# Moving the addition of a rotary embedding from GpSimd to VectorE

## The chip, the cores and the metric

The kernel runs on one core of a Trainium2 chip. The metric is the device time of one execution in microseconds (us). Before the change it was 1877.25 us, the median of three runs (1873.11 to 1878.32).

The engines of the core are called by their names here and by short names in the rows: TensorE (PE, its weight loads PEld), VectorE (DVE), ScalarE (ACT), GpSimd (POOL) and SyncE (SP, which only issues transfers; its queue is SPq).

## The reference, cut to what matters

The model is a "macaron": a feed-forward block, an attention block and the same feed-forward block again, on 2048 tokens of 128 features.

```python
x = x + 0.5 * ffn(layernorm(x), ...)    # ffn = attention with rope, then a mixture of 8 experts (top 2)
x = x + attn(layernorm(x), ...)         # attention with rope
x = x + 0.5 * ffn(layernorm(x), ...)

# in each of the three, with 16 heads of 8 features:
q, k, v = h @ wq, h @ wk, h @ wv
q = q * cos + rotated(q) * sin          # the rotation: two products and their sum; k likewise
scores = q @ k.T / sqrt(8)              # causal
out = softmax(scores) @ v
```

So all three layers contain the same attention, and the rotation (two products, one sum) stands in each.

## The kernel before, in words

The kernel loops three times over one body (layer 0, 1, 2). One pass has a head, the attention itself and, in layers 0 and 2, the experts.

**The head** works on four chunks c of 512 tokens. TensorE turns the normalised tokens (line 776) and multiplies them by four weight matrices, for q, q with its halves exchanged, k and k exchanged (line 785), and by the matrix for v (line 793). There are 8 items i = 2c + which, where which is 0 for q and 1 for k. Each item is a tile of 128 rows (head and feature) by 512 tokens. It is rotated, and then split into three bf16 parts, whose sum carries nearly the precision of f32, so that TensorE can form the scores in bf16. For item i the steps are:

1. two multiplies by VectorE (line 581): out of PSUM, plus a bias, times the table of cosines or sines, into two f32 tiles `terms(i)`, of which there are four pairs in turn;
2. the addition of the two by GpSimd (line 684), which signals `rotated`;
3. rounding the sum to bf16 by ScalarE (line 742), part 0;
4. the remainder, sum minus part 0, by VectorE (line 571, function `remainder`);
5. rounding the remainder by ScalarE (line 725, `second`), part 1;
6. remainder minus part 1 by GpSimd (line 678, `third`), part 2, which signals `part2_ready`.

Each engine executes its instructions in the order written. VectorE does the multiplies of item i and then remainder i - 2. GpSimd does addition i and then third part i - 2. ScalarE does second i - 2 and then part 0 of item i; between them it copies the turned tokens (line 729) and v (line 744) out of PSUM. From item 4 on VectorE waits for third part i - 4 before it writes `terms(i)`, as these tiles are used again.

SyncE stores the parts of chunk c to HBM, q (line 500) after third part 2c and k (lines 502 and 504) after third part 2c + 1. From the second chunk on it then loads chunk c - 1 back in the layout of the attention, with six transfers (line 385). So the load of chunk 0 stands behind the stores of chunk 1. The load of chunk 3 stands behind the first maxout (below).

**The attention** follows a list of events that a planner writes out before, from assumed costs; all engines walk the same list, and the change touches neither its costs nor its order. Its first events are row maxima: scores by TensorE (lines 821 and 824, which wait for the load of chunk 0 and for the v copy) and a maximum by VectorE (line 609). After all of a chunk's maxima comes "maxout": TensorE transposes them (line 830), VectorE splits them into three bf16 parts (lines 624 to 628), and they go through HBM into three rows of the operand qa. Then come the scores (line 867), the exponentials (ScalarE, line 759) and the products with v (line 880). The tiles `m3` and `mr` that the maxout writes lie in the same memory as `terms`. GpSimd, when its third parts are done, clears the guard rows of the second operand buffer (line 691).

Of the kernel before, what the change touches and what calls it, by code (L numbers as in the profile page):

```python
# [8 lines left out]
ALU = mybir.AluOpType  # L9
# [9 lines left out]
NC = T // CH  # L19
# [147 lines left out]
def macaron_kernel(nc, x_in, w5, b4, vecs, wo_w, rope, router, w_gate, w_up, w_down, out):  # L167
# [16 lines left out]
    def tmp(n):  # L184
        return arena[:, n * CH:(n + 1) * CH]
# [77 lines left out]
    def sem(name):  # L263
        s = nc.alloc_semaphore(name)
        sems.append(s)
        return s
# [14 lines left out]
    terms_ready = sem("terms_ready")  # L281
    rotated = sem("rotated")
# [3 lines left out]
    part2_ready = sem("part2_ready")  # L286
# [78 lines left out]
    def terms(i):  # L365
        return tmp(2 * (i % 4)), tmp(2 * (i % 4) + 1)

    def parts(i):
        return pbuf[i % PB].bitcast(BF16).rearrange("p (l t) -> p l t", l=3)
# [100 lines left out]
    with nc.Fori(0, NLAYER) as layer:  # L470

        with nc.Block() as block:
# [73 lines left out]
            def _(dve):  # L546
# [21 lines left out]
                def remainder(i):  # L568
                    rotation, rest = terms(i)
                    dve.wait_ge(part0_ready, i + 1)  # L570
                    dve.tensor_tensor(rest, rotation, parts(i)[:, 0, :], ALU.subtract).then_inc(remainder_ready, 1)

                for i in range(2 * NC):
                    c, which = i // 2, i % 2
                    if which == 0:
                        dve.wait_ge(table_loaded[c], 16)
                    if i >= 4:
                        dve.wait_ge(part2_ready, i - 3)
                    for k in (0, 1):
                        dve.wait_ge(projected, 2 * i + k + 1)  # L580
                        dve.scalar_tensor_tensor(terms(i)[k], ps[:, 2 + 2 * which + k, :],
                                                 b4s[:, 2 * which + k:2 * which + k + 1], rtab[:, k, c * CH:(c + 1) * CH],
                                                 ALU.add, ALU.mult).then_inc(terms_ready, 1)
                    if i >= 2:
                        remainder(i - 2)
                remainder(2 * NC - 2)
# [12 lines left out]
                for ev in events:  # L599
                    kind = ev[0]  # L600
                    if kind in ("rowmax", "maxout", "normalise", "turn", "project"):
                        bank = SB + mi % MB
                        mi += 1
                        dve.wait_ge(filler_ready, mi)
                    if kind == "rowmax":
                        _, j, qt, h0, some, kc, final = ev
                        g, c = chunks[j]
                        w = min(CH, (TPC * c + qt + 1) * 128 - kc * CH)
                        dve.tensor_reduce(mpart[:, j % MD, h0:h0 + some, qt, kc],  # L609
                                          ps[:, bank, 0:some * w].rearrange("p (h w) -> p h w", h=some),  # L610
                                          axis=AX.X, op=ALU.max).then_inc(filler_used, 1)
                        if final:
                            dve.wait_ge(filler_used, mi)
                            if j >= MD:
                                dve.wait_ge(guard_split, j - MD + 1)
                            dve.tensor_reduce(mx[:, j % MD, :], mpart[:, j % MD, :, :, 0:c + 1].rearrange("p h q c -> p (h q) c"), axis=AX.X,
                                              op=ALU.max, negate=True).then_inc(maxima_ready, 1)
                    elif kind == "maxout":

                        j = ev[1]  # L620
                        if j >= MD:
                            dve.wait_ge(guard_ready[j % MD], 16 * (j // MD))
                        src = ps[0:16, bank, 0:128]
                        link(dve.tensor_copy(m3[:, j % MD, 0, :], src))
                        dve.tensor_tensor(mr, src, m3[:, j % MD, 0, :], ALU.subtract).then_inc(filler_used, 1)
                        dve.wait_ge(filler_used, mi)
                        link(dve.tensor_copy(m3[:, j % MD, 1, :], mr))
                        dve.tensor_tensor(m3[:, j % MD, 2, :], mr, m3[:, j % MD, 1, :],
                                          ALU.subtract).then_inc(guard_split, 1)
                    elif kind == "normalise":  # L630
                        j = ev[1]
                        g, c = chunks[j]
                        turned = ps[:, bank, :].rearrange("p (q h r) -> p q h r", q=TPC, r=32)
                        link(dve.reciprocal(rden[:, :, :, :], turned[:, :, :, HD:HD + 1]))  # L634
                        dve.tensor_tensor(
                            onat[:, TPC * c:TPC * (c + 1), 32 * g:32 * g + 32].rearrange("p q (h i) -> p q h i", i=HD),
                            turned[:, :, :, 0:HD], rden[:, :, :, :].broadcast_to([128, TPC, HPG, HD]),
                            ALU.mult).then_inc(filler_used, 1)
                        dve.wait_ge(filler_used, mi)
                        dve.engine_nop().then_inc(output_normalised, 1)  # L640
                    elif kind == "turn":
                        c = ev[1]
                        dve.tensor_scalar(hT[:, c * CH:(c + 1) * CH], ps[:, bank, :], wos[:, D:D + 1], None,
                                          ALU.add).then_inc(filler_used, 1)
                    elif kind == "project":
                        c = ev[1]
                        rows = slice(TPC * c, TPC * (c + 1))
                        y = rec[:, 0, :].rearrange("p (t d) -> p t d", d=D)
                        dve.tensor_tensor(y, ps[:, bank, :].rearrange("p (t d) -> p t d", d=D),
                                          vbc[:, V_BO:V_BO + 1, :].broadcast_to([128, TPC, D]),  # L650
                                          ALU.add).then_inc(filler_used, 1)
                        dve.wait_ge(filler_used, mi)

                        if c == 0:
                            dve.wait_ge(x1_ready, TT)
                        with dve.If(layer == 1):
                            dve.tensor_tensor(xs[:, rows, :], xs[:, rows, :], y, ALU.add).then_inc(residual_added, 1)
                            dve.wait_ge(residual_added, c + 1)
                            for t in range(TPC * c, TPC * (c + 1)):
                                dve.bn_stats(stats[:, t, :], xs[:, t, :]).then_inc(stats_ready, 1)  # L660
                            dve.wait_ge(stats_ready, TPC * (c + 1))
                            for t in range(TPC * c, TPC * (c + 1)):
                                dve.bn_aggr(mv[:, t, :], stats[:, t, :]).then_inc(squares_done, 1)
                        with dve.If(layer != 1):
                            dve.tensor_tensor(x1[:, rows, :], x1[:, rows, :], y, ALU.add).then_inc(residual_added, 1)
                            dve.wait_ge(residual_added, c + 1)
                            for k in range(TPC):
                                t = TPC * c + k
                                dve.tensor_tensor_reduce(rec[:, 1, k * D:(k + 1) * D], x1[:, t, :], x1[:, t, :],
                                                         1.0, 0.0, ALU.mult, ALU.add, rst[:, 2, t:t + 1]  # L670
                                                         ).then_inc(squares_done, 1)
                        dve.wait_ge(squares_done, TPC * (c + 1))

            @block.gpsimd
            def _(pool):
                def third(i):
                    pool.wait_ge(part1_ready, i + 1)
                    pool.tensor_tensor(parts(i)[:, 2, :], terms(i)[1], parts(i)[:, 1, :],
                                       ALU.subtract).then_inc(part2_ready, 1)

                for i in range(2 * NC):
                    rotation, other = terms(i)
                    pool.wait_ge(terms_ready, 2 * i + 2)
                    pool.tensor_tensor(rotation, rotation, other, ALU.add).then_inc(rotated, 1)
                    if i >= 2:
                        third(i - 2)
                third(2 * NC - 2)
                third(2 * NC - 1)

# [7 lines left out]
                for ev in events:  # L697
                    if ev[0] == "scores":
                        _, s, j, kt, h = ev
# [614 lines left out]
```

## Time and profile before

| | |
|---|---|
| profiled execution | 1875.36 us |
| its span (first to last instruction) | 1873.8 us |
| TensorE busy | 1660.0 us, 89% |
| VectorE busy | 1364.7 us, 73% |
| ScalarE busy | 1104.4 us, 59% |
| GpSimd busy | 441.7 us, 24% |
| mean granted TensorE clock | 0.914 of full |

How to read it: the shares are means over the whole span, and the head of a layer is a short stretch of it (the first is at 12 to 44 us), so the rows below look at that stretch alone. The busy time of an instruction includes what it waits for inside the engine, such as memory that another engine holds. "Idle before" in brackets is how long the engine had nothing to do and what ended it. The granted clock is the share of TensorE's full speed that the chip allowed.

### The profile page before, as it was taken

The page shows a single profiled execution, that of the slowest core. Times are in us where ns is not written, and L with a number is a line of the kernel's source. Part 1 is how long each engine was busy: PE and PEld are TensorE (multiplying, and loading weights), DVE is VectorE, ACT ScalarE, POOL GpSimd, SP SyncE. Part 2 cuts the span into 40 slices and gives each one's busy share as a digit, 9 for nine tenths or more (in the row PEclk, how much of TensorE's full clock was granted, in tenths as well). Part 3 has the DMA queues.
Part 4 walks back from the last instruction along what each step waited for, and adds up shares of the span by engine and source line. Part 5 has one row for each costly group of instructions (what it writes and reads, how often), then busy time and mean ns, then how long its engine had stood idle before and what let it go on. Part 6 is the DMA issues. An engine that isn't in the chain of part 4 may idle for free. (4 is left out here: it accounts for less than half of the span.)

```text
span 1873.8 us, 31585 instructions
## 1 busy us (share of the span) xinstructions
PE 1660.0 (89%) x11190; PEld 769.0 (41%) x11190; DVE 1364.7 (73%) x2862; ACT 1104.4 (59%) x2304; POOL 441.7 (24%) x491
## 2 busy tenths in 40 slices
PE   5899999999849947899999999579999999994795
PEld 3333333333239933333333332233333333423795
DVE  7888998987153348889999983388899999825333
ACT  5355777767716624457777778234576777782463
POOL 6003201111016735031101020150311010200574
PEclk9788999999959977889999999778899999995898
DMA  5400203300011134200202000142002020001113
GB/s 163 108 1 3 52 3 105 68 2 2 8 33 44 47 100 141 52 2 2 53 2 52 2 2 2 61 141 52 2 7 47 2 53 2 1 2 30 35 47 89
DMA packets 63581, 75.92 MB, mean 41 GB/s; under 512 B 13656, under 2 KB 56221, under 8 KB 62105
## 3 DMA queue, kind: packets, MB, share of 16 engines
q1 hardware_dynamic: 54184, 62.13, 13.1%
q0 software_dynamic: 4992, 9.40, 2.1%
q10 hardware_dynamic: 4224, 2.10, 0.4%
q8 instruction: 99, 1.62, 0.4%
q14 instruction: 82, 0.66, 0.1%
HBM read 53.05 MB, written 21.46 MB: 40 GB/s over the span
## 5 line engine op out<-in xcount | busy, mean ns | idle before, releaser
L759 ACT ACTIVATE probs<-ps 128x512 f32<-128x512 f32 (+3 forms) x1920 | 879.0, 543 | 471.3 <-PE ps L867 469.8
L609 DVE TENSOR_REDUCE mpart<-ps 128x1 f32<-128x512 f32 (+3 forms) x1680 | 1014.4, 665 | 115.6 <-PE ps L821 65.3
L821 PE MATMUL ps<-ka,qa 96*128 96x512 bf16 (+3 forms) x1920 | 669.6, 371 | 36.5 <-DMA ka<-ksplit 23.1
L867 PE MATMUL ps<-qa,ka 96*128 96x512 bf16 (+3 forms) x1920 | 616.2, 357 | 1.5 <-DMA qa<-guard 0.9
L880 PE MATMUL ps<-probs,vv 128*9 128x512 f32 (+3 forms) x3840 | 442.5, 533 | 8.8 <-ACT probs L759 8.1
L708 POOL TENSOR_SCALAR_AFFINE_SELECT probs<-probs 128x512 f32<-128x512 f32 x192 | 122.0, 635 | 1168.7 <-ACT probs L759 1168.7
L821 PEld LDWEIGHTS ps<-ka,qa 96*128 96x128 bf16 x1920 | 191.8, 100 | 480.3 <-DVE mpart L609 335.6
L867 PEld LDWEIGHTS ps<-qa,ka 96*128 96x128 bf16 x1920 | 183.4, 99 | 187.7 <-ACT probs L759 69.2
L824 PE MATMUL ps<-mask_rows,identb 128*128 128x128 bf16 x768 | 161.6, 235 | 0.0
L1215 DVE TENSOR_TENSOR probs<-probs,ps 112x512 f32<-112x512 f32 x78 | 53.6, 687 | 144.5 <-ACT probs L1183 144.5
L1140 PE MATMUL ps<-hT,probs 128*112 128x128 f32 x1248 | 152.7, 277 | 2.9 <-ACT probs L1170 1.9
L1140 PEld LDWEIGHTS ps<-hT,probs 128*112 128x112 f32 x1248 | 144.9, 180 | 4.2 <-ACT probs L1170 2.2
L880 PEld LDWEIGHTS ps<-probs,vv 128*9 128x9 f32 x3840 | 57.7, 88 | 158.4 <-ACT probs L759 118.3
L1170 ACT ACTIVATE probs<-wgu 128x896 f32 x78 | 74.1, 950 | 66.4 <-PEq L886 38.5
L1074 POOL DMA_INDIRECT arena<-tokens,from_row x78 | 76.9, 986 | 115.7 <-issue 69.5
L634 DVE RECIPROCAL rden<-ps 128x16 f32<-128x16 f32 x48 | 11.9, 249 | 113.2 <-PE ps L835 113.0
L1084 POOL DMA_INDIRECT results<-hT,to_row x78 | 78.5, 1007 | 59.3 <-issue 30.7
L824 PEld LDWEIGHTS ps<-mask_rows,identb 128*128 128x128 bf16 x768 | 80.3, 105 | 28.9 <-issue 2.0
L1152 PE MATMUL ps<-wds,probs 112*128 x624 | 82.8, 275 | 1.5 <-DVE probs L1215 1.4
L1152 PEld LDWEIGHTS ps<-wds,probs 112*128 112x128 f32 x624 | 75.8, 192 | 2.3 <-issue 2.3
L1163 ACT ACTIVATE hT<-ps 128x128 f32<-128x128 f32 x78 | 21.6, 277 | 61.6 <-PE ps L1124 61.6
L776 PE MATMUL ps<-identf,onat 128*128 128x128 f32 x48 | 9.1, 321 | 54.2 <-DVE onat L562 54.2
(166 smaller groups left out, 943.6 us busy)
## 6 DMA issues: line engine op xcount, KB each, us to landing
qa<-qsplit SPq DMA_DIRECT2D x27, 384.0 KB
ka<-ksplit SPq DMA_DIRECT2D x27, 384.0 KB
probs<-rope SPq DMA_DIRECT2D x12, 512.0 KB, 6.3
qa<-qsplit SPq DMA_DIRECT2D x36, 96.0 KB
ka<-ksplit SPq DMA_DIRECT2D x36, 96.0 KB
qsplit<-arena SPq DMA_DIRECT2D x6, 384.0 KB, 3.0
ksplit<-arena SPq DMA_DIRECT2D x6, 384.0 KB, 2.8
tokens<-arena SPq DMA_DIRECT2D x2, 1024.0 KB, 8.0
```

Source lines behind the costliest of these rows:

```text
L609: dve.tensor_reduce(mpart[:, j % MD, h0:h0 + some, qt, kc], ps[:, bank, 0:some * w].rearrange("p (h w) -> p h w", h=some), axis=AX.X, op=A ...
L708: pool.affine_select(out=own, in_=own, compare_op=ALU.is_ge, fill=0.0, base=0, pattern=[[0, HPG], [1, 128]], channel_multiplier=-1).then_i ...
L759: act.activation(probs[:, s % 2, h, 0:n], ps[:, u % SB, 0:n], ACT.Exp, scale=SCALE).then_inc(probs_ready, 1)
L821: ins = pe.matmul(dst, qa[0:KROWS, b, h0 + k, tile * 128:(tile + 1) * 128], ka[0:KROWS, b, h0 + k, kc * CH:kc * CH + n], start=True, stop= ...
L824: ins = pe.matmul(dst[:, n - 128:n], identb[:, :], mask_rows[:, :], start=False, stop=True)
L867: pe.matmul(dst, ka[0:KROWS, b, h, kt * 128:(kt + 1) * 128], qa[0:KROWS, b, h, c * CH + q0:(c + 1) * CH], start=True, stop=True).then_inc( ...
L880: ins = pe.matmul(ps[32 * h:32 * h + HD + 1, SB + MB, q0:CH], vv[:, kt, g * HPG + h, :], probs[:, s % 2, h, 0:CH - q0], start=kt == 0, sto ...
L1074: pool.indirect_dma_start(xring[:, u % XR, :], None, tokens, bass.IndirectOffsetOnAxis(ap=from_row[:, u:u + 1], axis=0)).then_inc(tile_loa ...
L1084: pool.indirect_dma_start(results, bass.IndirectOffsetOnAxis(ap=to_row[:, u:u + 1], axis=0), obuf[:, u % OR, :], None, bounds_check=TOPK * ...
L1140: ins = pe.matmul(ps[0:MR, 2 * (i % 2) + b, k * 128:(k + 1) * 128], wcur[:, i % 2, b * M + k * MR:b * M + (k + 1) * MR], xt[:, i % 2, :], ...
L1152: ins = pe.matmul(ps[:, 4 + u % 2, 0:D], atb[u % 2][:, k * 128:(k + 1) * 128], wds[0:MR, bass.ds(experts[u], 1), k, :].rearrange("p o d -> ...
L1170: act.activation(wcur[:, u % 2, :], wgu[:, bass.ds(expert, 1), :].rearrange("p o m -> p (o m)"), ACT.Copy).then_inc(expert_copied, 1)
```

## The change: what it does

VectorE executes the addition itself, right behind the two multiplies of the same item, after a wait for its own second multiply. GpSimd loses the addition and executes only the eight third parts. Since the order of GpSimd no longer guarantees that third parts are done before the maxout overwrites the memory of `terms`, VectorE waits for all eight before the first maxout. ScalarE, TensorE and SyncE have the same instructions and waits as before.

```diff
--- before.py
+++ after.py
@@ -581,6 +581,9 @@
                         dve.scalar_tensor_tensor(terms(i)[k], ps[:, 2 + 2 * which + k, :],
                                                  b4s[:, 2 * which + k:2 * which + k + 1], rtab[:, k, c * CH:(c + 1) * CH],
                                                  ALU.add, ALU.mult).then_inc(terms_ready, 1)
+                    rotation, other = terms(i)
+                    dve.wait_ge(terms_ready, 2 * i + 2)
+                    dve.tensor_tensor(rotation, rotation, other, ALU.add).then_inc(rotated, 1)
                     if i >= 2:
                         remainder(i - 2)
                 remainder(2 * NC - 2)
@@ -618,6 +621,8 @@
                     elif kind == "maxout":
 
                         j = ev[1]
+                        if j == 0:
+                            dve.wait_ge(part2_ready, 2 * NC)
                         if j >= MD:
                             dve.wait_ge(guard_ready[j % MD], 16 * (j // MD))
                         src = ps[0:16, bank, 0:128]
@@ -678,12 +683,8 @@
                     pool.tensor_tensor(parts(i)[:, 2, :], terms(i)[1], parts(i)[:, 1, :],
                                        ALU.subtract).then_inc(part2_ready, 1)
 
-                for i in range(2 * NC):
-                    rotation, other = terms(i)
-                    pool.wait_ge(terms_ready, 2 * i + 2)
-                    pool.tensor_tensor(rotation, rotation, other, ALU.add).then_inc(rotated, 1)
-                    if i >= 2:
-                        third(i - 2)
+                for i in range(2 * NC - 2):
+                    third(i)
                 third(2 * NC - 2)
                 third(2 * NC - 1)
```

## Rows read from the trace of the kernel before

**Rows 1.** the page, part 1: busy us (share of span), instructions.

```profile
PE 1660.0 (89%) x11190; PEld 769.0 (41%) x11190; DVE 1364.7 (73%) x2862; ACT 1104.4 (59%) x2304; POOL 441.7 (24%) x491
```

**Rows 2.** windows: length; busy of PE, PEld, DVE, ACT, POOL; granted clock; DMA.

```profile
27.30:45.20 17.90, 9.94 (x45) 6.04 (x44) 14.28 (x14) 11.12 (x18) 17.63 (x14) 0.84 0.64 195
...
44.00:60.00 16.00, 12.91 (x59) 5.84 (x60) 13.97 (x27) 0.96 (x1) 4.63 (x3) 0.61 0.74 198
60.00:600.00 540.00, 493.66 (x3340) 211.90 (x3338) 404.17 (x831) 333.11 (x712) 95.76 (x116) 0.92 0.14 32
```

**Rows 3.** timeline: start, duration, engine, line, operation [idle before]; heads of layers 0, 1.

```profile
17.36 0.75 DVE L581 SCALAR_TENSOR_TENSOR arena<-ps,b4s,probs 128x512 f32<-128x512 f32 x1 [0.45 <-PE ps L785]
...
44.26 0.26 PE L821 MATMUL ps<-ka,qa 96*128 96x128 bf16 x1 [7.96 <-DMA ka<-ksplit]
...
695.78 0.75 DVE L581 SCALAR_TENSOR_TENSOR arena<-ps,b4s,probs 128x512 f32<-128x512 f32 x1 [0.44 <-PE ps L785]
...
722.69 0.26 PE L821 MATMUL ps<-ka,qa 96*128 96x128 bf16 x1 [7.56 <-DMA ka<-ksplit]
```

**Rows 4.** timeline of SyncE's queue in the head of layer 0.

```profile
36.45 0.36 SPq L502 DMA_DIRECT2D ksplit<-x  x1
...
40.06 0.38 SPq L385 DMA_DIRECT2D ka<-ksplit  x1
...
46.30 0.38 SPq L385 DMA_DIRECT2D ka<-ksplit  x1
```

**Rows 5.** timeline of GpSimd in the head of layer 0.

```profile
27.33 1.16 POOL L678 TENSOR_TENSOR arena<-arena 128x512 bf16<-128x512 f32 x1 [0.95 <-ACT arena L725]
28.45 1.27 POOL L684 TENSOR_TENSOR arena<-arena 128x512 f32<-128x512 f32 x1
...
32.48 1.15 POOL L678 TENSOR_TENSOR rec<-arena,rec 128x512 bf16<-128x512 f32 x1
...
35.27 1.16 POOL L678 TENSOR_TENSOR x<-arena,x 128x512 bf16<-128x512 f32 x1
...
43.97 1.15 POOL L678 TENSOR_TENSOR rec<-arena,rec 128x512 bf16<-128x512 f32 x1
```

**Rows 6.** timeline of ScalarE in the head of layer 0.

```profile
26.63 0.62 ACT L725 ACTIVATE arena<-arena 128x512 bf16<-128x512 f32 x1
...
34.22 0.63 ACT L725 ACTIVATE x<-arena 128x512 bf16<-128x512 f32 x1 [1.03 <-DVE arena L571]
...
41.45 0.58 ACT L744 ACTIVATE vv<-ps 128x512 f32<-128x512 f32 x1
```

**Rows 7.** by line, whole span: count, duration ns min/median/max, first and last start.

```profile
L684 POOL TENSOR_TENSOR arena<-arena x24: 1264/1680/1727, 19.8 to 1230.1; 128x512 f32<-128x512 f32 x24
...
L678 POOL TENSOR_TENSOR x<-arena,x x6: 1144/1150/1167, 35.3 to 1229.0; 128x512 bf16<-128x512 f32 x6
...
L571 DVE TENSOR_TENSOR arena<-arena x12: 678/1114/1748, 24.6 to 1230.6; 128x512 f32<-128x512 f32 x12
...
L581 DVE SCALAR_TENSOR_TENSOR arena<-ps,b4s,probs x48: 732/743/752, 17.4 to 1228.5; 128x512 f32<-128x512 f32 x48
```

**Rows 8.** timeline of VectorE in the head of layer 0.

```profile
25.16 1.40 DVE L581 SCALAR_TENSOR_TENSOR arena<-ps,b4s,probs 128x512 f32<-128x512 f32 x2
26.48 0.68 DVE L571 TENSOR_TENSOR arena<-arena 128x512 f32<-128x512 f32 x1
28.58 1.41 DVE L581 SCALAR_TENSOR_TENSOR arena<-ps,b4s,probs 128x512 f32<-128x512 f32 x2 [1.42 <-POOL arena L678]
...
32.62 1.55 DVE L571 TENSOR_TENSOR arena<-arena,x 128x512 f32<-128x512 f32 x1
```

**Rows 9.** timeline of the first maxout in layer 0.

```profile
51.89 0.27 PE L830 MATMUL ps<-identf,mx 128*16 128x128 f32 x1 [1.65 <-DVE mx L616]
...
52.20 0.28 DVE L624 CAST arena<-ps 16x128 bf16<-16x128 f32 x1 [0.45 <-PE ps L830]
52.51 0.28 DVE L625 TENSOR_TENSOR arena<-ps,arena 16x128 f32<-16x128 f32 x1
```

## The prediction

> **What bounds the kernel now.** I read the page first: TensorE carries 89% of the span [rows 1], so the kernel is TensorE's. The edited code, though, runs only in the head of each of the three layers, before the attention. The table by windows says what such a stretch looks like: in the 17.9 us from 27.3 GpSimd is busy 17.63 and VectorE 14.28, TensorE only 9.94, while in 60 to 600 TensorE has 493.66 of 540 [rows 2]. So only the end of the head matters. The timeline shows where it lies: in layer 0 the first product of the attention starts at 44.26 after 7.96 idle, released by the load of a piece of ka; in layer 1 it starts at 722.69. Counted from the first product with the rope table (17.36 and 695.78) that is 26.90 and 26.91 us [rows 3]; the third layer repeats it. The head is thus a fixed number, paid three times, and nothing in front of that wait covers a delay: TensorE has no other work.
>
> What fixes 26.90? Walk back from 44.26. The last load of chunk 0 is issued at 40.06, six issues after the store of k of chunk 1 at 36.45 [rows 4], because SyncE's order puts that store in front. This store waits for the fourth third part (i = 3), which GpSimd computes from 35.27 to 36.43 [rows 5]. So the price of the change is read at one point: when "third(3)" ends. Behind it come a fixed 0.02, the stores, six issues and the landing, 7.83 us in all up to 44.26, which the change leaves alone. The other condition of the first product, v copied out, is met at 41.45 + 0.58 = 42.03 [rows 6], 2.2 us early.
>
> Now the pace up to third(3). GpSimd alternates between the addition for i and the third part for i - 2. Third parts 2 and 3 start at 32.48 and 35.27, a period of 2.79 [rows 5]. By line, the third part takes 1.15, the addition a median of 1.68 but a minimum of 1.26; VectorE's remainder takes between 0.68 (minimum) and 1.55, and its multiply out of PSUM 0.74, always [rows 7, 8]. Two engines stretch each other there. The timeline shows how: remainder 1 at 26.48, with GpSimd idle, takes 0.68. Remainder 3 starts at 32.62, while third part 2 runs from 32.48 to 33.63, and ends at 34.17, that is 0.54 after GpSimd is through [rows 5, 8]. The addition at 28.45, beside VectorE's multiplies from 28.58, takes 1.27, near its minimum [rows 5, 8]. So two-input work on SBUF of one engine waits for the other's, and the multiply from PSUM waits for nobody. The period now is the sum of what is serialised: 1.15 + 1.12 (an addition without its wait: 1.68 less 0.54 of the remainder) + 0.54 = 2.81, against 2.79 seen.
>
> **The change part by part.** *Removed:* 8 additions a layer on GpSimd. GpSimd keeps one instruction of 1.15 a period and is no longer the bound.
>
> *Added:* 8 additions a layer on VectorE, same shape as the remainder: 0.68 alone; behind another VectorE instruction 0.60, since the pair of multiplies takes 1.40 for two of 0.74 (0.08 overlap) [rows 7, 8]; 0.54 after GpSimd's end if it had to wait. Before each stands a wait for VectorE's own multiply. The nearest rows of such a wait are the link of the maxima: the copy at 52.20 ends at 52.48, the next starts at 52.51 [rows 9]: 0.03 instead of an overlap of 0.08.
>
> The new period, counted from the end t of a remainder. The two multiplies take 1.40 and start some 0.07 before t, by the overlap seen where remainder 1 starts at 26.48 and the multiplies from 25.16 end at 26.56 [rows 8]; so they end at t + 1.33. The addition could start at t + 1.36. But ScalarE starts rounding the remainder at t + 0.05 (34.22 after 34.17) and takes 0.63 [rows 6]; GpSimd's third part follows 0.08 later (26.63 + 0.62, then 27.33) [rows 5, 6], so from about t + 0.75 to t + 1.90. The addition arrives in the middle of it, waits, and ends at t + 1.90 + 0.54 = t + 2.44; the next remainder follows at t + 3.04. The new period is 3.04, 0.25 longer than 2.79: VectorE now does what GpSimd did and also waits for the third part once a period. The bounds of this period are 2.64 (no wait: 1.33 + 0.03 + 0.68 + 0.60) and about 3.7 (the remainder waits instead of the addition, below). I take 3.04, as the rows give the start of the third part to about 0.05, well inside the addition's window.
>
> The start. Addition 2 and remainder 0 push VectorE's multiplies for i = 3 from 25.16 [rows 8] by one addition, 0.65, to 25.8; they end at 27.2, and addition 3 wants the port at 27.24. Third part 0 starts at 27.33 as before, because ScalarE's rounding at 26.63 stood behind ScalarE's own queue and not behind the remainder. The two meet within 0.1; whoever is first, remainder 1 ends near 28.49 + 0.54 + 0.60 = 29.63 (before: 26.48 + 0.68 = 27.16). Remainder 3 is two periods on, 35.71, and third part 3 ends at 35.71 + 1.90 = 37.61. Before: 36.43. **The difference is 1.18 us a layer, 3.5 us in three.** GpSimd's relief buys nothing, because each third part now hangs on VectorE's string of four instructions.
>
> What else moves. TensorE's projections wait for these multiplies, but they end before third part 3 in both orders, and the v copy moves to about 43.5, before the new first product at 45.4. Third part 7 moves from 45.12 (43.97 + 1.15) [rows 5] to about 46.5, so the stores of chunk 3 and loads of chunks 1 to 3 move by as much. The last load of chunk 1 is issued at 46.30 [rows 4], the work that needs it comes after the maxima's transpose at 51.89 [rows 9]; both shift by nearly the same, and the slack of 5.6, less a landing of 4.2 as for chunk 0, stays 1.4 or so. I cost that at nothing; if this cover were gone, it costs the difference of the two shifts, 0.2 a layer. The new wait in front of the first maxout, for all 8 third parts, is met at 46.5 and asked at about 53: nothing; behind it on VectorE stand the row maxima. GpSimd's memset of the guard rows moves 1.4 later, and the load that asks for it comes after the second maxout.
>
> The Trainium skill, "SBUF — State Buffer", section "SBUF: two separate sides", says that VectorE and GpSimd share one pair of ports under an exclusive lock, that a VectorE instruction with two SBUF inputs takes it, and that the loser blocks for the whole instruction. This trace agrees (0.54 after the other's end). It speaks against this change: by it the period is the 3.04 above; by durations alone it would be 2.64.
>
> **The rivals.**
> (a) *The waits disappear and VectorE simply is the faster adder* (0.68 against 1.27). For it: the third part takes 1.15 and the multiplies 1.33 of each period, so they could lie side by side. Against: the rounding on ScalarE puts 0.75 in front of the third part. With 2.64, remainder 1 ends at 28.5, remainder 3 at 33.8, third part 3 at 35.7: 0.7 earlier a layer, 2.2 in all. Near 1875, within 0.3% still.
> (b) *Slower: the third part slips between addition and remainder.* It decides where the rounding starts over 0.6 us late, because ScalarE is held by a copy out of PSUM (0.58 [rows 6]); then the third part starts after t + 1.36, the addition is through, and the remainder waits for all of it: 1.36 + 0.60 + 1.15 + 0.54 = 3.65 a period. Remainder 3 ends at 36.9, third part 3 at 38.8 or, late itself, 39.4: 2.4 to 3.0 a layer, about 8 in all, 1885. Against it: ScalarE is busy 11.12 of 17.90 in that stretch [rows 2], and its long copies lie beside the multiplies.
> (c) *The granted clock in the attention.* It was 0.61 of full in 44 to 60 and 0.92 in 60 to 600 [rows 2]. The head's shift may move the drops; one per cent over TensorE's 493.66 is 5 us a layer, either way. Nothing in the profile favours one sign.
> (d) *The load's landing hides the shift.* The last issue at 40.06 is 4.2 before the first product [rows 3, 4], long for a transfer; were it set by other traffic, the shift would vanish: no change.
>
> **How the numbers follow.** The profiled execution took 1875.36, 1.56 more than its span, and plus 3.5 gives 1878.9. The median of the runs shown is 1877.25, 1.9 above that execution; from the median I forecast 1877.25 + 3.5 = 1880.8. What a measurement of this kernel can tell from no change is about 0.3%, 5.6 us. Chances: the forecast 0.50 (within 0.3%); (a) and (d) together 0.18 (within); (b) 0.18 (slower); (c) 0.07 faster, 0.07 slower. So faster 0.07, same 0.68, slower 0.25. The range runs from (a) with the runs' spread below it, 1874, to (b) with some above it, 1887.
>
> **What would show it.** Right: the additions stand on VectorE 24 times with a minimum of 0.68 and a usual 1.08 (waiting); the third parts 1 to 4 of a layer lie 3.0 apart; the first product of the attention starts 28.1 after the first multiply instead of 26.9, still released by the load of ka; GpSimd's busy time falls by some 38 us (24 x 1.6), VectorE's rises by about 25; from there on all stages are as before. Wrong: third parts 2.7 apart or less is (a); remainders of 1.7 and additions of 0.7 is (b); a head as long as before is (d); equal heads plus 4 us and a different total is (c).

## The result and the profile after

The changed kernel took 1884.61 us, the median of 8 runs (1880.37 to 1888.27), against 1875.28 us for 8 runs of the kernel before (1873.11 to 1878.32). The ratio is 1.0048, with a 95% interval of 1.0035 to 1.0060: slower by 9.3 us in this comparison, where I had forecast 3.5. Two more comparisons, below, gave 1.0018 and 1.0023. The profiled execution took 1880.37 us, the lowest of its eight, 5.0 over the profiled execution before.

By engine the page after has (to compare with [rows 1]):

```profile
span 1878.5 us, 31588 instructions
...
PE 1661.6 (88%) x11190; PEld 769.3 (41%) x11190; DVE 1375.4 (73%) x2886; ACT 1103.3 (59%) x2304; POOL 405.0 (22%) x467
```

GpSimd's busy time fell by 36.7 us (I had said 38). VectorE's rose by only 10.7 (I had said 25): the additions brought 21.4, but six of the eight remainders of a layer now take 0.68 (before, two), and all 24 together fell from 32.0 to 20.8. In the head of layer 0 the table by windows (length; busy of PE, PEld, DVE, ACT, POOL; clock; DMA) shows GpSimd idle half the time, where it had been full [rows 2], and the head still longer:

```profile
27.30:47.00 19.70, 11.09 (x50) 6.66 (x50) 16.95 (x22) 11.28 (x20) 9.79 (x9) 0.84 0.59 185
```

The additions and third parts by line (they answer to L684 and L678 in [rows 7]; line 586 is the addition now, 683 the third part):

```profile
L586 DVE TENSOR_TENSOR arena<-arena x24: 691/889/1102, 19.8 to 1232.4; 128x512 f32<-128x512 f32 x24
```

```profile
L683 POOL TENSOR_TENSOR x<-arena,x x6: 1152/1152/1153, 37.0 to 1231.8; 128x512 bf16<-128x512 f32 x6
```

The timeline of VectorE in the head of layer 0 (to compare with [rows 8]) is the mechanism:

```profile
26.49 1.40 DVE L581 SCALAR_TENSOR_TENSOR arena<-ps,b4s,probs 128x512 f32<-128x512 f32 x2
27.93 0.69 DVE L586 TENSOR_TENSOR arena<-arena 128x512 f32<-128x512 f32 x1
28.54 1.64 DVE L571 TENSOR_TENSOR arena<-arena 128x512 f32<-128x512 f32 x1
...
33.16 1.40 DVE L581 SCALAR_TENSOR_TENSOR arena<-ps,b4s,probs 128x512 f32<-128x512 f32 x2
34.59 1.09 DVE L586 TENSOR_TENSOR arena<-arena 128x512 f32<-128x512 f32 x1
35.60 0.68 DVE L571 TENSOR_TENSOR arena<-arena,x 128x512 f32<-128x512 f32 x1
```

And GpSimd beside it [rows 5], and the chain to the first product [rows 3, 4]:

```profile
33.97 1.15 POOL L683 TENSOR_TENSOR rec<-arena,rec 128x512 bf16<-128x512 f32 x1 [1.89 <-ACT rec L726]
37.02 1.15 POOL L683 TENSOR_TENSOR x<-arena,x 128x512 bf16<-128x512 f32 x1 [1.89 <-ACT x L726]
```

```profile
38.20 0.36 SPq L502 DMA_DIRECT2D ksplit<-x  x1
...
41.84 0.38 SPq L385 DMA_DIRECT2D ka<-ksplit  x1
```

```profile
45.63 0.27 PE L822 MATMUL ps<-ka,qa 96*128 96x128 bf16 x1 [8.55 <-DMA ka<-ksplit]
```

Read them together. The multiplies end at 34.56, the addition follows 0.03 later, but third part 2 runs from 33.97 to 35.12. The addition is not through before 35.68, 0.56 after GpSimd's end, having taken 1.09 instead of 0.69. The third parts start 3.05 apart (3.04 forecast, 2.79 before). Third part 3 ends at 38.17 instead of 36.43, SyncE's store leaves 0.03 later, the last load at 41.84, and the first product comes at 45.63 instead of 44.26.

The heads of all three layers, from the first multiply to the first product of the attention, read from the same two kinds of row in each profile (us). "Before with the new wait" and "null" are experiments below:

| kernel, profiled execution | layer 0 | layer 1 | layer 2 | sum less 80.7 |
|---|---|---|---|---|
| before, first | 26.90 | 26.91 | 26.88 | 0.0 |
| before, again ("null") | 26.98 | 26.80 | 26.83 | -0.1 |
| before with the new wait | 26.60 | 27.16 | 26.61 | -0.3 |
| changed, first | 28.27 | 27.18 | 27.59 | +2.3 |
| changed, second | 28.32 | 27.97 | 27.30 | +2.9 |
| changed, third | 28.57 | 28.41 | 27.73 | +4.0 |

The heads of one kernel differ by over 1 us, so they are a coarse measure. A part of them is sharp: from the start of the multiplies for i = 2 to the end of third part 3. These two rows, of the kernel before and of the changed one, give its start in layer 0:

```profile
23.10 1.54 DVE L581 SCALAR_TENSOR_TENSOR arena<-ps,b4s,probs 128x512 f32<-128x512 f32 x2 [1.66 <-PE ps L785]
```

```profile
23.71 1.54 DVE L581 SCALAR_TENSOR_TENSOR arena<-ps,b4s,probs 128x512 f32<-128x512 f32 x2 [0.93 <-PE ps L786]
```

That is 36.43 - 23.10 = 13.33 us before and 38.17 - 23.71 = 14.46 after. In all nine heads of either kind in the table it is 13.32 or 13.33 before and 14.46 to 14.49 after. So the change costs 1.15 us a layer in this chain, 3.4 in three layers. What is left of the head scatters whatever the kernel: in these six profiles the way to the multiplies for i = 2 took 5.4 to 6.6 us (the last section says why), and the way from third part 3 to the first product 7.2 to 8.0.

### The profile page after: what moved, and what is told of

Read it like the earlier page. It is cut to its first block and busy times, and to the rows that moved or that the text cites. A ratio compares the mean times of both kernels' runs of the same rounds, so it can differ in the third digit from the quotient of the medians.

```text
span 1878.5 us, 31588 instructions
## 1 busy us (share of the span) xinstructions
PE 1661.6 (88%) x11190; PEld 769.3 (41%) x11190; DVE 1375.4 (73%) x2886; ACT 1103.3 (59%) x2304; POOL 405.0 (22%) x467
```

## The experiments

Every ratio is to the kernel before, run on the same chip. It is the ratio on record with its interval, and can differ a little from the quotient of the two medians (1.0023 against 1.0035 in the third comparison of the changed kernel). On one of the chips all kernels were slower (before: 1908.65 us there), so only ratios are compared. The heads and layer 1 were as long there as elsewhere; the extra time lay behind the heads of layers 0 and 2 (672.1 and 652.0 us, against 651.5 and 638.9).

**The kernel before against itself, and the changed kernel again.** No edit.

> The kernel before, unchanged, timed against itself: ratio 1.000, with an interval of about 0.1 to 0.2 per cent. Its second profile tells how much a stretch between two landmarks (first product of the attention in one layer to the first multiply of the next: 651.5, 485.3, and 639.0 to the end) differs from run to run. If the attention's length varies by about 2 us a layer by itself, the rest of the measured 9.3 us beyond the heads may be chance or clock; if it repeats within 0.5 us, the change does something in the attention that I have not named.

Measured: 1907.54 us, ratio 0.9994 (0.9980 to 1.0009). The attention and what follows it in layer 1, from its first product to the next layer's first multiply, took 485.1 us in this profile and 485.3 in the first one; but 489.1 in the kernel with only the new wait, which did not lose time by it (below). So the stretches behind the heads can differ by some 4 us between single profiles. This goes with the granted clock: over all 13 profiles, ten with 484.3 to 488.2 us in this stretch had TensorE at the lower of its two levels for 64.5 to 71.8 us of it, and the three with 489.1 to 491.6 for 76.3 to 79.5.

> The changed kernel again, unchanged. Theory A (the longer head is all there is; it cost 1.4, 0.3 and 0.7 us in the profiled run): ratio 1.001 to 1.003, plus 2 to 5 us. Theory B (something beyond the heads, at least as large): ratio 1.004 to 1.006 again, plus 8 to 10 us. The head of a layer, from the first multiply to the first product of the attention, is 27.2 to 28.3 us.

Measured: 1912.07 us, ratio 1.0018 (1.0002 to 1.0034). The heads are 2.9 us longer in sum. Theory A: by the ratio it is 3.4 us. On this chip the stretches behind the heads add up to 1809.8 us in the changed kernel's profile and to 1809.3 in that of the kernel before, so between these two profiles the heads are nearly all of it.

> The changed kernel a third time, for the size of the loss. The first comparison gave 1.0048 (1.0035 to 1.0060), the second 1.0018 (1.0002 to 1.0034); the heads of the two profiled executions add up to 2.4 and 3.0 us more than before, ratio 1.0013 to 1.0016. If the heads are all, 1.001 to 1.003 again; if the changed kernel loses something elsewhere that these two profiles do not show, 1.004 or more.

Measured: 1881.63 us against 1875.14, ratio 1.0023 (1.0009 to 1.0037), heads 4.0 us longer. By the ratio that is 4.3 us. So the two repeats, 3.4 and 4.3 us, match the heads of their own profiles (2.9 and 4.0) and the 3.4 of the chain, as far as intervals of some 3 us either way can say; only the first comparison, 9.3 us beside heads of 2.3, does not. Weighted by their intervals the three give 1.0032, some 6 us, but they differ by more than their intervals allow (1.0035 to 1.0060 against 1.0002 to 1.0034), so something varies between comparisons that the intervals don't contain, and this mean is not known to 0.001.

**A delay of the same place, without the change.** The kernel before, and on GpSimd:

```diff
                 def third(i):
+                    if i == 3:
+                        pool.memset(<128 rows of qa, buffer 1>[:, 0:1400], 0.0)   # or [:, 0:4096]
                     pool.wait_ge(part1_ready, i + 1)
```

> The kernel before with one memset of 3.5 us on GpSimd in front of third part 3 of each layer; nothing else. It lengthens the head by about 3.5 us and moves no work between engines. Theory A (a head's delay passes one to one): plus 10.5 us, ratio 1.0056. Theory B' (a later start costs more than itself, through clock or lost overlap in the attention): plus 14 us or more. Partly hidden: less than 8.

Measured: 1920.18 us, ratio 1.0055 (1.0036 to 1.0074), heads 30.60, 30.29 and 30.68: 10.9 us in sum; the time, by the ratio, plus 10.5. The chain from the multiplies to third part 3 is 3.45 us longer in each layer. So a delay in the head passes one to one, as far as the interval can tell (6.9 to 14.1 us).

> The kernel before with a memset of 1.2 us on GpSimd in front of third part 3 of each layer. This is the change's delay without its move of work: third part 3 comes 1.2 us later. If a head's delay is the whole mechanism, this kernel and the changed one lose the same, 3.6 us (ratio 1.002), and the heads are 28.1. If the changed kernel is over this one by more than 3 us, something else is in it. If small delays are absorbed, 1.000.

Measured: 1882.55 us, ratio 1.0032 (1.0018 to 1.0046), beside 1.0023 for the changed kernel in the same runs. The timeline of GpSimd says how large the delay came out:

```profile
35.01 1.26 POOL L678 MEMSET qa<- 128x1400 f32 x1
36.23 1.15 POOL L680 TENSOR_TENSOR x<-arena,x 128x512 bf16<-128x512 f32 x1
37.35 1.26 POOL L686 TENSOR_TENSOR arena<-arena 128x512 f32<-128x512 f32 x1
```

The heads were 27.56, 27.39 and 27.54, only 1.8 us over before in sum, not 3.6. The delay itself is there in full: the chain from the multiplies for i = 2 to third part 3 takes 14.52 us instead of 13.32, 1.20 a layer. But this execution reached those multiplies early (5.5, 5.4 and 5.4 us after the first one, before 5.8, 6.2 and 6.1; in layer 0 third part 0 began at 27.08 and not at 27.33). It was also the fastest of its twelve, 1873.44 us, so its heads don't stand for the median. What can be said is that a kernel that is only late at this place, by as much as the changed one, loses as much (1.0032 and 1.0023, within their intervals). The 3.6 us lie just inside the interval of this one (3.4 to 8.6).

**The lock.** The changed kernel, with GpSimd as busy at the same moments but reading nothing (the third part of the split is left out, zeros are stored):

```diff
-                    pool.tensor_tensor(parts(i)[:, 2, :], terms(i)[1], parts(i)[:, 1, :], ALU.subtract)...
+                    if i < 7:
+                        pool.memset(<128 rows of qa, buffer 1>[:, (i % 3) * 1350:(i % 3 + 1) * 1350], 0.0)
+                    pool.memset(parts(i)[:, 2, :], 0.0).then_inc(part2_ready, 1)
```

> The changed kernel, but GpSimd writes zeros instead of the third parts: a memset of 1350 columns of a free buffer (about 1.15 us, for the first seven items) and one of the part, so it is as busy at the same moments and reads no SBUF. The third part of the split is left out. Lock theory (the addition waits because GpSimd's subtraction reads SBUF through what VectorE's second input needs): every addition takes 0.69 and the period of the remainders falls from 3.04 to 2.64 to 2.70. Rival (any GpSimd instruction beside a two-input one of VectorE stretches it): additions stay at about 1.09 or more, the period at 3.0 or more. Rival (VectorE's string is slow by itself): period stays 3.0 with additions of 0.69.

One execution: 1881.35 us, against a median of 1877.26 for before. A single time decides nothing here; the trace does. The additions by line:

```profile
L586 DVE TENSOR_TENSOR arena<-arena x24: 691/691/693, 19.7 to 1231.5; 128x512 f32<-128x512 f32 x24
```

and the timelines of GpSimd and VectorE:

```profile
33.70 1.22 POOL L684 MEMSET qa<- 128x1350 f32 x1 [1.51 <-ACT rec L728]
34.87 0.52 POOL L686 MEMSET rec<- 128x512 bf16 x1
```

```profile
32.30 0.68 DVE L571 TENSOR_TENSOR arena<-arena,rec 128x512 f32<-128x512 f32 x1
32.90 1.40 DVE L581 SCALAR_TENSOR_TENSOR arena<-ps,b4s,probs 128x512 f32<-128x512 f32 x2
34.34 0.69 DVE L586 TENSOR_TENSOR arena<-arena 128x512 f32<-128x512 f32 x1
34.95 0.68 DVE L571 TENSOR_TENSOR arena<-arena,x 128x512 f32<-128x512 f32 x1
```

All 24 additions take 0.69, among them the one from 34.34 in the middle of a memset that runs from 33.70 to 34.92. The remainders are 2.65 apart (32.30 to 34.95), not 3.05. Both rivals fall: VectorE's string alone would be fast enough, and a GpSimd that is busy but reads nothing does not stop the addition. The Trainium skill, "SBUF — State Buffer", section "SBUF: two separate sides", says just this: two SBUF inputs on VectorE contend only with a GpSimd operation that reads SBUF. The head isn't shorter here (27.6 to 28.3). Two memsets end 1.7 us after they begin and not 1.15, which leaves the chain from the multiplies for i = 2 to third part 3 at 13.8 us, 0.7 under the changed kernel but 0.5 over before; and this execution's first projections were slow (see the last section).

**The new wait alone.** The kernel before, plus `if j == 0: dve.wait_ge(part2_ready, 2 * NC)`.

> The kernel before with only the change's new wait in front of the first maxout. It is asked at about 52 us and met at 45.1, so ratio 1.000 within 0.15 per cent and heads as before (26.9). If it cost something, the loss beyond the heads would show here: 1.002 or more.

Measured: 1877.13 us against 1877.26, ratio 1.0000 (0.9988 to 1.0012). It costs nothing that can be measured (0.1%, 2 us, would show).

**The same move with the other order.** The changed kernel, with VectorE's order turned:

```diff
-                    rotation, other = terms(i)
-                    dve.wait_ge(terms_ready, 2 * i + 2)
-                    dve.tensor_tensor(rotation, rotation, other, ALU.add).then_inc(rotated, 1)
                     if i >= 2:
                         remainder(i - 2)
+                    rotation, other = terms(i)
+                    dve.wait_ge(terms_ready, 2 * i + 2)
+                    dve.tensor_tensor(rotation, rotation, other, ALU.add).then_inc(rotated, 1)
```

> The changed kernel with VectorE's order turned: remainder i - 2 before addition i. If the head is lengthened by the addition's wait for GpSimd's third part, the period falls from 3.04 to 2.64 (multiplies 1.33, remainder and addition 1.28, the third part beside the multiplies), third part 3 ends about 1.7 us earlier in each layer, and the head is 26.3 to 26.6 us: 0.3 to 0.5 shorter than before the change. Theory A then gives a time of 1 to 2 us under before (ratio 0.999), theory B, where the loss comes from something the changed kernel does elsewhere, leaves it over before by 4 us or more. If VectorE's load in itself is the cause, the head stays over 27 us.

> The changed kernel with the remainder in front of the addition, again. The first comparison gave 0.9983 (0.9964 to 1.0001) with heads 1.8 us shorter in all than before; so 0.998 to 1.000, and below the changed kernel by 0.25 to 0.5 per cent.

Measured: 0.9983 (0.9964 to 1.0001) the first time, with heads of 27.43, 25.18 and 26.17 us, and 0.9981 (0.9971 to 0.9992) the second time, in the same runs in which the changed kernel had 1.0023; heads 27.67, 26.97 and 25.73, 0.3 under before in sum. The heads scatter too widely to test the 26.3 to 26.6 that I expected. The chain from the multiplies for i = 2 to third part 3 does it: 12.74 to 12.76 us in all six, 1.7 under the changed kernel as expected and 0.6 under the kernel before. The timelines of the first one in layer 0, GpSimd and then VectorE:

```profile
33.09 1.16 POOL L683 TENSOR_TENSOR rec<-arena,rec 128x512 bf16<-128x512 f32 x1 [1.90 <-ACT rec L726]
35.54 1.16 POOL L683 TENSOR_TENSOR x<-arena,x 128x512 bf16<-128x512 f32 x1 [1.29 <-ACT x L726]
38.06 1.16 POOL L683 TENSOR_TENSOR x<-arena,x 128x512 bf16<-128x512 f32 x1 [1.36 <-ACT x L726]
```

```profile
35.32 1.40 DVE L581 SCALAR_TENSOR_TENSOR arena<-ps,b4s,probs 128x512 f32<-128x512 f32 x2
36.64 0.67 DVE L571 TENSOR_TENSOR arena<-arena,x 128x512 f32<-128x512 f32 x1
37.24 0.68 DVE L588 TENSOR_TENSOR arena<-arena 128x512 f32<-128x512 f32 x1
```

The third part from 35.54 to 36.70 now lies beside the multiplies from 35.32 to 36.72, which take nothing from it, and remainder and addition run at 0.67 and 0.68. The period is 2.5 instead of 3.05 (2.64 expected). The same instructions on the same engines, in another order, turn the loss into a gain: the loss was the place of the third part and not the load on VectorE. (The first interval still touches 1, the second doesn't.)

**What the end of the head hangs on.** SyncE's order changed, on the kernel before and on the turned one:

```diff
+                    if c:
+                        load_first(c - 1)
                     sp.wait_ge(part2_ready, 2 * c + 2)
                     <store k of chunk c>
-                    if c:
-                        load_first(c - 1)
```

> The kernel before with one change on SyncE: the load of chunk c - 1 is issued after the store of q of chunk c and no longer after that of k. If the head ends with the load of chunk 0, which waits for third part 3 only by this order, the load's issues start at about 34.5 instead of 37.5 in layer 0, and the first product comes when v is copied out (42.1) instead of 44.3: 2.2 us less a layer, 6.6 in all, ratio 0.9965. Rival (the landing of that load is set by other traffic, so the order does nothing): ratio 1.000, head 26.9.

> Both: VectorE adds, remainder in front of addition, and the load of chunk c - 1 issued behind the store of q. In the swapped kernel third part 3 came 0.7 to 1.7 us earlier a layer than before the change and v was copied out earlier too. Theory: heads of 24 to 25 us, 2 to 3 us less a layer than before, ratio 0.995 to 0.997, and the best of all. Rival: the v copy or the last multiply is the limit in both, so no better than early alone.

Measured, in the same runs: before with the early load 1871.49 us, ratio 0.9971 (0.9958 to 0.9983), heads 25.11, 24.40 and 25.26, 5.9 us less in sum (6.6 expected); turned with the early load 1872.92 us, ratio 0.9975 (0.9966 to 0.9984), heads 24.75, 23.47 and 23.66, 8.8 less. The first product with the early load alone:

```profile
42.47 0.26 PE L821 MATMUL ps<-ka,qa 96*128 96x128 bf16 x1 [5.83 <-ACT vv L744]
```

The releaser is now the v copy, at 42.47 (42.1 forecast). So before the change it was SyncE's order that tied the head's end to third part 3, as the prediction read it. Both versions beat both kernels. Between the two there is no difference that can be told, although one has heads 2.9 us shorter in its profile; my expectation that both together would be the best of all is not borne out. The stretch of its layer 1 behind the head took 491.6 us, with early alone 489.3; these are two of the three profiles with the long time at the lower clock level. Whether an earlier head brings that about isn't shown.

## Why the prediction was right, and where not

- *The bound (the end of third part 3, by way of SyncE's order).* Shown: the early load removes that link and 5.9 us of head, and a memset in front of third part 3 passes in full. But the head is not "a fixed number, paid three times", and the 7.83 behind third part 3 is not fixed either. Before, the three heads were 5.75 + 13.32 + 7.83, 6.16 + 13.32 + 7.43 and 6.08 + 13.32 + 7.49 us (to the multiplies for i = 2, to the end of third part 3, to the first product). Only the middle term is fixed; that the sums agreed to 0.02 was luck.
- *The period of 3.04.* Measured 3.05, with the addition waiting in the middle of the third part, as described. The lock in it is shown by the memsets. The sum for the period before has a slip: 1.68 less 0.54 is 1.14, not 1.12. With the 1.72 that these additions take in rows of the steady state, 1.15 + 0.54 + 1.14 less an overlap of 0.04 gives the 2.79 seen; nothing in the forecast hangs on it. The start was as worked out up to the collision: addition 3 came first (27.93), the third part started at 27.94 and took 1.70, and remainder 1 waited for it.
- *The head, +1.18 a layer.* Right, and sharper than the heads themselves say: they were +1.37, +0.27 and +0.71 in the first profile, 1.0 on average over three profiles, but the chain up to third part 3 is 1.13 to 1.17 longer in all nine, 1.15 on average. In layer 0 the end of third part 3 was 38.17 and not 37.61. Those 0.56 are not the change's: the projections of the first chunk took 6.11 us instead of 5.50, and everything after started 0.6 later.
- *The tail and the new wait at nothing.* Right as far as it shows: 1.0000 for the wait. The first maxout's transpose came 1.4 later as the first product did.
- *The additions, "minimum 0.68, usually 1.08".* Only 12 of 24 waited (median 0.89, maximum 1.10); the first four of a layer meet an idle GpSimd or come before it.
- *The total.* 1880.8 forecast, 1884.6 measured, inside the range. The outcome fell in the case "slower by over 0.3%", to which I gave 0.25, and not in "within 0.3%", 0.68. Luck helped: 1880.8 started from 1877.25, the median of three runs, and the median of eight is 1875.28. As a difference, 3.5 us were forecast and 9.3 measured. The step that did not hold in this comparison is the last one, that the heads' sum is the difference in time. In the two repeats it held (3.4 and 4.3 us).
- *The rivals.* (a) is excluded by the waits of 1.09, (d) by the first product that moved with the last load's issue, and (b) because no remainder waited behind an addition in the steady state. Rival (c), the granted clock, finds no support either: the mean granted clock over the timed runs was 0.9138 for the changed kernel and 0.9144 for before in the second comparison, 0.9133 and 0.9134 in the third. Within the runs of the kernel before, 0.01 of it goes with 10 to 13 us, so these differences are worth less than 1 us and 0.1 us. For the first comparison the clock of the runs before is not on record. What made up the further 6 us of that comparison stays open; its profiled execution, 4.7 longer in span than the one before, has 2.3 of them in the heads and 2.4 behind (-2.1, +2.0 and +2.5 by layer), which is within the scatter of single profiles.

## What to carry to other kernels

Before moving work from GpSimd to VectorE, look at what both read: here the two-input work of both on SBUF tiles was serialised wherever it met (where VectorE had to wait, it ended 0.54 to 0.56 us after GpSimd), so a lighter GpSimd may gain nothing, and what counts is whether the remaining GpSimd operation falls beside VectorE work out of PSUM. If it doesn't, try the order of VectorE's instructions first; one swapped pair was worth 0.4% here. And where a stage ends with a transfer, ask which queue order holds it: moving six issues ahead of one wait gained 0.3%, the moved additions in their better order 0.2%. Last, look for the part of a stage that repeats to 0.03 us and price the change there; whole heads, and single profiles of long stretches, scattered by as much as the 3.4 us in question.

## What was not expected of the hardware

TensorE's first projections change their pace in the middle, and not always at the same time. The timeline of weight loads, of the kernel before and then of the changed one, in layer 0:

```profile
17.87 0.34 PEld L785 LDWEIGHTS ps<-hT,otf 128*128 128x128 f32 x1 [0.52 <-issue]
18.73 0.24 PEld L785 LDWEIGHTS ps<-hT,otf 128*128 128x128 f32 x1 [0.52 <-issue]
19.20 0.19 PEld L785 LDWEIGHTS ps<-hT,otf 128*128 128x128 f32 x1 [0.24 <-issue]
```

```profile
18.72 0.34 PEld L786 LDWEIGHTS ps<-hT,otf 128*128 128x128 f32 x1 [0.52 <-issue]
19.57 0.34 PEld L786 LDWEIGHTS ps<-hT,otf 128*128 128x128 f32 x1 [0.52 <-issue]
20.24 0.19 PEld L786 LDWEIGHTS ps<-hT,otf 128*128 128x128 f32 x1 [0.33 <-issue]
```

The spacing falls from 0.85 to 0.43, and the load from 0.34 to 0.19. But it does so at about 18.8 in the one and 20.0 in the other, after identical work from 15.15 and 15.14 on. Over the profiles the eight projections took 5.12 to 6.78 us. In layer 0 the table by windows seems to deny that this is the granted clock, which reads 1.00 in both from 12 to 21 us:

```profile
19.00:20.00 1.00, 1.00 (x3) 1.00 0.96 332
```

```profile
19.00:20.00 1.00, 1.00 (x2) 1.00 0.89 242
```

Layer 1 shows that it is the clock all the same. There the same fall of the load from 0.34 to 0.19 stands beside a granted clock that rises from 0.50 to 1.00, from TensorE's lower level to its higher (windows and weight loads of the kernel before):

```profile
697.00:698.00 1.00, 1.00 (x2) 0.50 1.01 375
698.10:699.00 0.90, 0.90 (x4) 1.00 0.97 361
```

```profile
697.16 0.34 PEld L785 LDWEIGHTS ps<-hT,otf 128*128 128x128 f32 x1 [0.52 <-issue]
698.48 0.19 PEld L785 LDWEIGHTS ps<-hT,otf 128*128 128x128 f32 x1 [0.24 <-issue]
```

In layer 0 the trace's records of the clock begin only at 18.82 us before and at 20.04 after the change, just where the pace changes, and the table counts the time ahead of the first record as full speed. So what varies from profile to profile is the moment at which the granted clock rises: in layer 0 between 18.32 and 21.37 us over the 13 profiles, with the same work from 15.15 on. A head of 27 us carries up to 1.7 us of this, more than the term that was to be predicted, and one profile of a changed kernel is a poor measure of a whole head.
